# Attention input of a graph transformer: expert rows added to x inside the gather transfers, in two groups of eight, with two x buffers

## The reference, cut to what matters

```
x = x + gnn0(layernorm(x), adj)
x = x + moe(layernorm(x))           # a shared expert + the top 2 of 8 experts per node
x = x + attention_gnn(layernorm(x), adj)
x = x + slicing_attention(layernorm(x))

# attention_gnn, 4 heads of 32:
X, q, k = heads(leaky(x @ W_lin + b)), heads(leaky(x @ W_q)), heads(leaky(x @ W_k))
adj_h = adj * sigmoid(q k^T / sqrt(32));  deg = sum(adj_h, -1)
dis = where(deg > 0, deg ** -0.5, 0)
Y = dis * adj_h * dis @ X;  out = layernorm(Y) * ln_g + ln_b
```

## Time and profile before

| | |
|---|---|
| median of 3 runs | 1789.09 us (1788.44 to 1789.14) |
| the profiled execution's own time | 1787.95 us |
| its span | 1786.2 us |
| TensorE, VectorE busy | 1534.8 us, 1054.1 us of the span |
| ScalarE, GpSimd busy | 702.1 us, 717.3 us |
| mean granted TensorE clock | 0.928 of full speed |
| attention stage in the span | from about 730 to 1330 us |

### The profile page before, as it was taken

One profiled execution on the slowest core, in us unless ns is written; L12 is line 12 of the kernel. 1 busy time (PEld: TensorE's weight loads), 2 busy tenths in 40 slices (PEclk: granted clock), 3 DMA queues, 4 the chain that ended last, 5 costly groups with the idle time before them and its releaser, 6 DMA issues. The chain is left out here.

```text
span 1786.2 us, 25017 instructions
## 1 busy us (share of the span) xinstructions
PE 1534.8 (86%) x9208; PEld 834.3 (47%) x9208; DVE 1054.1 (59%) x2248; ACT 702.1 (39%) x978; POOL 717.3 (40%) x501
## 2 busy tenths in 40 slices
PE   5899997996999999237999989999958999967598
PEld 2355555655766677212222222222215777743278
DVE  2467774411232222139899989998957887825612
ACT  3365645332333333025555545556502343412110
POOL 1137776400000000379878777842225565610000
PEclk9899998998999999669999999999977898979799
DMA  9676643555555554223334333333220000020214
GB/s 281 219 254 218 210 133 93 163 128 135 151 146 141 142 151 120 73 82 114 113 100 125 99 108 115 104 106 97 83 61 24 22 15 23 1 84 1 47 56 136
DMA packets 214663, 199.86 MB, mean 112 GB/s; under 512 B 22529, under 2 KB 176513, under 8 KB 214546
## 3 DMA queue, kind: packets, MB, share of 16 engines
q1 hardware_dynamic: 206354, 181.46, 34.4%
q0 software_dynamic: 8192, 16.86, 2.9%
HBM read 150.17 MB, written 48.10 MB: 111 GB/s over the span
## 5 line engine op out<-in xcount | busy, mean ns | idle before, releaser
L1249 DVE TENSOR_TENSOR c_AH<-c_AH,c_A 128x2048 f32<-128x2048 f32 x128 | 314.9, 2469 | 38.5 <-ACT c_AH L1218 37.7
L1218 ACT ACTIVATE c_AH<-c_S 128x2048 f32<-128x2048 f32 x128 | 240.6, 1880 | 226.4 <-PE c_S L1116 226.4
L687 ACT ACTIVATE a_A<-a_DG,a_A 128x512 f32<-128x512 f32 x220 | 150.7, 687 | 275.8 <-PE a_DG L561 271.2
L1065 POOL DMA_INDIRECT c_G<-ys,slots x128 | 223.7, 1748 | 44.1 <-issue 41.0
L561 PE MATMUL a_DG<-a_A 128*128 128x512 f32 x440 | 216.3, 615 | 7.0 <-ACT a_A L687 7.0
L1116 PE MATMUL c_S<-c_Q,c_K 32*128 32x512 f32 x1024 | 151.5, 662 | 23.8 <-DVE c_K L1306 12.9
L444 POOL DMA_INDIRECT rows<-a_S,a_slots x128 | 134.6, 1051 | 56.2 <-issue 42.9
L1049 POOL MEMSET c_power<- 128x32 f32 x1 | 0.1, 124 | 388.5 <-issue 388.5
L1141 PE MATMUL c_DG<-c_AH,c_ones 128*32 128x512 f32 x1024 | 139.9, 619 | 16.4 <-DVE c_AH L1249 16.3
L1129 PE MATMUL c_YA<-c_AH,c_XT 128*32 128x512 f32 x1024 | 137.1, 617 | 7.2 <-DVE c_XT L1274 7.2
L561 PEld LDWEIGHTS a_DG<-a_A 128*128 128x128 f32 x440 | 75.7, 192 | 107.1 <-ACT a_A L687 79.0
(11 more groups left out here) (314 smaller groups left out, 2413.1 us busy)
## 6 DMA issues: line engine op xcount, KB each, us to landing
a_A<-in_dram SPq DMA_DIRECT2D x32, 1024.0 KB, 9.7
c_A<-in_dram SPq DMA_DIRECT2D x128, 256.0 KB
a_A<-in_dram SPq DMA_DIRECT2D x40, 514.0 KB, 3.4
a_A<-rows SPq DMA_DIRECT2D x39, 258.0 KB, 3.7
ys<-a_A SPq DMA_DIRECT2D x39, 256.0 KB, 2.3
rows<-a_zero SPq DMA_DIRECT2D x16, 258.0 KB, 9.2
a_X<-in_dram SPq DMA_DIRECT2D x8, 512.0 KB, 13.3
a_R<-in_dram SPq DMA_DIRECT2D x8, 512.0 KB, 4.7
```

The source lines that it names most:

```text
L687: act.activation(hT[g % 2][:, f, :], UP[f % 2], ACT.Gelu, bias=w_of(g)[:, F_N + f:F_N + f + 1]).then_inc(h_ready, 1)
L1065: pool.indirect_dma_start(Gt[k][:, t, :], None, ys, bass.IndirectOffsetOnAxis(ap=slots[:, k, T * i + t:T * i + t + 1], axis=0), bounds_che ...
L1218: act.activation(AH[g % UNITS][:, :, :], S[:, :, :], ACT.Sigmoid, scale=HD ** -0.5).then_inc(att_ready, 1)
L1249: dve.tensor_tensor(ah[:, :, :], ah[:, :, :], A[g % ADJ_BUFS][:, :].unsqueeze(1).to_broadcast([P, HEADS, HALF]), ALU.mult).then_inc(ah_dve, 1)
```

## The change

Each gather adds the rows that it fetches to X in the transfer (`compute_op=ALU.add`). `Gt` and the two additions of `combine` are gone. A transfer that adds reads X and writes it back, so the eight gathers of a graph's first expert wait for the load of X, and the eight of the second expert wait for the first eight. X has two buffers, taken in turn, each with its own semaphores for loading and storing; `load_x(i + 2)` moves from step 11 to step 1, and the loads of graphs 0 and 1 stand first in SP's queue. On GpSimd the first eight gathers of graph i + 2 stand after root(i - 1, 1), the second eight after root(i, 0). VectorE's statistics and `keep_x` wait for the sixteen gathers where they waited for the addition.

```diff
-        X, Y, R = sb("X", [P, T, D]), sb("Y", [P, T, D]), sb("R", [P, T, D])
-        Gt = [sb(f"G{k}", [P, T, D]) for k in range(2)]
+        X = [sb(f"X{u}", [P, T, D]) for u in range(2)]
+        Y, R = sb("Y", [P, T, D]), sb("R", [P, T, D])
...
             def load_x(i):
-                if i > 0:
-                    sp.wait_ge(side_full, full["xn1", i - 1])
-                sp.dma_start(X[:, :, :], tiled(x_in[i])).then_inc(x_loaded, 16)
+                if i >= 2:
+                    sp.wait_ge(side_full, full["xn1", i - 2])
+                sp.dma_start(X[i % 2][:, :, :], tiled(x_in[i])).then_inc(x_loaded[i % 2], 16)
 
             def keep_x(i):
-                sp.wait_ge(x_ready, i + 1)
-                sp.dma_start(tiled(kept[i]), X[:, :, :]).then_inc(x_kept, 16)
+                sp.wait_ge(gathered, 256 * i + 256)
+                sp.dma_start(tiled(kept[i]), X[i % 2][:, :, :]).then_inc(x_kept[i % 2], 16)
 
             load_x(0)
+            load_x(1)
             for g in range(2):
                 load_adj(g)
             keep_x(0)
-            load_x(1)
...
-                    if n == 11 and is_graph(i + 2):
+                    if n == 1 and is_graph(i + 2):
                         load_x(i + 2)
...
-            def gather(i, part):
+            def gather(i, k, part):
                 if is_graph(i):
-                    wait(pool, x_ready, i)
-                    for m in part:
-                        k, t = divmod(m, T)
+                    pool.wait_ge(x_loaded[i % 2], 16 * (i // 2 + 1))
+                    wait(pool, gathered, 256 * i + 128 * k)
+                    for t in part:
                         pool.indirect_dma_start(
-                            Gt[k][:, t, :], None, ys,
+                            X[i % 2][:, t, :], None, ys,
                             bass.IndirectOffsetOnAxis(ap=slots[:, k, T * i + t:T * i + t + 1], axis=0),
-                            bounds_check=limit).then_inc(gathered, 16)
-
-            def combine(i):
-                pool.wait_ge(gathered, 256 * i + 256)
-                pool.tensor_tensor(Gt[0][:, :, :], Gt[0][:, :, :], Gt[1][:, :, :], ALU.add).then_inc(pair_ready, 1)
-                pool.wait_ge(pair_ready, i + 1)
-                pool.wait_ge(x_loaded, 16 * i + 16)
-                pool.tensor_tensor(X[:, :, :], X[:, :, :], Gt[0][:, :, :], ALU.add).then_inc(x_ready, 1)
-
-            gather(0, range(16))
-            combine(0)
+                            bounds_check=limit, compute_op=ALU.add).then_inc(gathered, 16)
+
+            gather(0, 0, range(T))
+            gather(0, 1, range(T))
             norm_in.power(pool, power, 0, 0)
-            gather(1, range(16))
-            combine(1)
+            gather(1, 0, range(T))
+            gather(1, 1, range(T))
             for i in range(B + 2):
-                gather(i + 2, range(4))
                 if is_graph(i + 1):
                     norm_in.power(pool, power, i + 1, (i + 1) % 2)
                 if is_graph(i - 1):
                     root(i - 1, 1)
-                gather(i + 2, range(4, 8))
+                gather(i + 2, 0, range(T))
                 if is_graph(i - 2):
                     pool.wait_ge(r_loaded, 16 * (i - 1))
                     pool.tensor_tensor(R[:, :, :], R[:, :, :], wide(shift), ALU.add).then_inc(shifted, 1)
                     norm_y.power(pool, power, i - 2, i % 2)
-                gather(i + 2, range(8, 16))
                 if is_graph(i):
                     root(i, 0)
-                if is_graph(i + 2):
-                    combine(i + 2)
+                gather(i + 2, 1, range(T))
...
             def stats_x(i):
-                dve.wait_ge(x_ready, i + 1)
-                norm_in.stats(dve, X, i, i % 2)
+                dve.wait_ge(gathered, 256 * i + 256)
+                norm_in.stats(dve, X[i % 2], i, i % 2)
 
             def apply_x(i):
-                dve.wait_ge(x_kept, 16 * i + 16)
-                norm_in.apply(dve, X, X, i, i % 2).then_inc(xn_ready, 1)
+                dve.wait_ge(x_kept[i % 2], 16 * (i // 2 + 1))
+                norm_in.apply(dve, X[i % 2], X[i % 2], i, i % 2).then_inc(xn_ready, 1)
```

More of the change, by code:

```diff
@@ L971, in attention_gnn_stage @@
         w_loaded, consts = sem("w_loaded"), sem("consts")
-        x_loaded, r_loaded, stored = sem("x_loaded"), sem("r_loaded"), sem("stored")
+        x_loaded = [sem(f"x_loaded{u}") for u in range(2)]
+        r_loaded, stored = sem("r_loaded"), sem("stored")
         adj_loaded = [sem(f"adj_loaded{b}") for b in range(ADJ_BUFS)]
@@ L975, in attention_gnn_stage @@
         norm_y = LayerNorm(lambda n, s: sb("y" + n, s), lambda n: sem("y" + n))
-        gathered, pair_ready, x_ready, x_kept = sem("gathered"), sem("pair_ready"), sem("x_ready"), sem("x_kept")
+        gathered = sem("gathered")
+        x_kept = [sem(f"x_kept{u}") for u in range(2)]
         xn_ready = sem("xn_ready")
@@ L1159, in side @@
                     for c in range(4):
-                        mm = pe.transpose(M[:, c * P:(c + 1) * P], X[:, 4 * half + c, :], ident[:, :])
+                        mm = pe.transpose(M[:, c * P:(c + 1) * P], X[i % 2][:, 4 * half + c, :], ident[:, :])
                 elif what[:-1] == "x":
```

## The result

The changed kernel takes 1810.53 us (median of 4 runs, 1807.26 to 1811.95) against 1789.12 before: a ratio of 1.0117, 95% interval 1.0100 to 1.0135. It is 1.2% slower. The forecast was 1779, faster; what came is rival (a), a dear adding gather, just inside the range. The profiled execution took 1810.76 us with a span of 1809.0, against 1787.95 and 1786.2.

The account below looks back on a forecast made before the run. TensorE sets a steady round's pace, 61.9 us, and GpSimd's additions cost about 6 us more through VectorE. Terms -25.4 + 0 - 2.7 + 15.6 + 2.0 = -10.5 us gave 1779 us, range 1764 to 1812.

Parts of the forecast that it names:

- rival (a): GpSimd's adding gathers issue 0.2 us or more above plain ones; 1802 us at 1.5; 33% together with slow landing.
- the price of an adding gather: GpSimd's issue of each adding gather: 1.05 us assumed, between bounds 1.01 and 2.06; +2.0 us in all.
- the estimate of 1.5 us: Issue time of one adding gather if it goes with the moves; the sum would come out at 1802 us.
- The additions: GpSimd's two additions for each graph block VectorE; removing them from six rounds gives -25.4 us.
- The start: Inputs of the first two graphs, gathered in two groups of eight: 0 us for graph 0, -2.7 us for graph 1.
- The order: Second eight gathers behind root(i, 0): VectorE stalls 5.5 us, TensorE loses 2.6 in each of six rounds, +15.6 us.
- Rival (b): In the rounds the gathers are in time or VectorE's idleness takes the whole stall: no +15.6, 1763 us; chance 15%.
- (c): No stall is absorbed, as TensorE also waits at side products: 17.4 us more, 1796 us; chance 12%.
- The price in the rounds: Each us more for an adding gather costs about 3.2 us in each of the six VectorE stalls.
- The sum: All terms over the whole kernel: -25.4 + 0 - 2.7 + 15.6 + 2.0 = -10.5 us.
- The shift's addition and root(i - 1, 1): On GpSimd, the addition now behind eight gathers and root(i - 1, 1) before them: cost 0 us.

Follow-up runs that it names:

- second_early: The changed kernel with all of the second eight gathers moved ahead of root(i, 0); 1798 us.
- spread: The changed kernel with the gather order of the kernel before, x of graph i + 3 being loaded at step 11; 1791.20 us.
- plain_price: The changed kernel with plain gathers in the same places and with the same waits, overwriting x instead of adding; 1777.65 us.

## Why the prediction was wrong

The step that failed is the price of an adding gather. I took 1.05 us because two forms of indirect DMA in the trace cost nearly the same, and neither of them adds. It is 1.56, 0.55 above a plain one; the prediction put the point from which this rival decides at 0.25. The Trainium skill (Collectives: The Full Stack, Stop ④ — SDMA + CCE) shows two reads and a write for an add; the estimate of 1.5 us that was worked out from it stands close to the 1.56 measured, its 1802 us 8.5 below the time. That issue time goes with the moves is not shown by this: it is one agreement, and nothing here varies the moves alone. The estimate was left out of the sum, and that was the weighing that went wrong: an operation in no row was priced by rows that share only its name.

Point by point, from the marks:

- **The additions**, -25.4 us forecast. 20.7 in the rounds (533.95 to 513.29). The block of VectorE is as forecast, but that four fifths came is in part luck. The sum counted each blocked us once, in every round; in the rounds of graphs 1, 2 and 5 only 1.0 to 1.9 us came, and of the 20.7 TensorE's idle time gave 11.3. The other 9.3 are its products at a higher granted clock, a term that the sum did not have.
- **The start**, -2.7 forecast. With plain gathers in the same order the marks say -4.5 (793.13 for 797.58), counted from the load of x -1.7: right in kind and near in size. The price adds 17.3 us counted so, and 32 x 0.55 = 17.6 is the issue alone: all of it is issue, as far as one profile of each can tell. +15.6 in all, +14.5 by the marks.
- **The order**, +15.6 forecast. At the plain price 529.34 - 513.29 = 16.1 us. The stall of VectorE, 5.5 forecast, was 3.8 to 5.2 in five of six rounds, and TensorE's waits behind them 1.0 to 2.6, 10.1 together, where 6 x 2.6 had been forecast; 4.6 of the 16.1 are longer busy time of TensorE (468.83 for 464.21). So the near agreement is in part luck as well. second_early and spread show by undoing it that the stall comes from the place of the gathers behind root(i, 0). Rival (b), no stall, falls with that, and (c), nothing absorbed, with the slack of 1.8 to 2.8 us in each stall.
- **The price in the rounds**, 19 us for each us: 10.5 expected for 0.55, 13.0 measured (542.36 less 529.34), of which 4.7 are again TensorE's busy time.
- **The sum** with 1.56 put in would have been -25.4 - 2.7 + 15.6 + 51 x 0.55 = +15.6 us; measured were +21.4 between the medians and +22.9 at the stage end. Most of the rest is what the additions' gain lacked (4.7) and the price in the rounds had more (2.5). In rival (a) the step from 1.05 to 1.5 us is written as 0.46 and is 0.45; 1802 stands.
- The shift's addition and root(i - 1, 1) were taken as free. No wait of VectorE names them in the steady rounds of the changed kernel, but a block shows as a longer instruction, not as a wait. In three of the four steady rounds the addition lengthens the output norm's step to 4.29 us from 2.18, much as it had lengthened the input's normalisation before. In round 3 it meets a leaky step (0.69 us elsewhere), and TensorE waits for the multiply behind it:

```profile
1025.93 3.74 DVE L1298 SCALAR_TENSOR_TENSOR c_XR<-c_XR 128x512 f32<-128x512 f32 x1
1026.23 2.88 POOL L1085 TENSOR_TENSOR c_R<-c_R,c_shift 128x1024 f32<-128x1024 f32 x1
1031.93 1.66 PE L1133 MATMUL c_DG<-c_AH,c_ones 128*32 128x512 f32 x8 [2.63 <-DVE c_AH L1241]
```

What stays open: the three marks rest on one profile each, so parts under about 2 us are not certain, and how much of TensorE's longer busy time each wait brings was not followed. Whether the 0.55 us are spent on reading the destination or on preparing a further transfer a row was not tried; no kernel here separates them.

What the Trainium skill (SBUF — State Buffer, Who interferes with whom) infers, that a multiply with two SBUF inputs does not hinder the issue of gathers, does not hold here. In the changed kernel, too, a gather that begins under a multiply takes 2.92 us (1128.55, above) where 1.56 is its price, and in the kernel before each of the 60 gathers that begin well inside one takes 1.67 us or more. Whether the gather's own read of `slots` in SBUF is what meets the multiply, no run here separates. An adding gather ends 1.43 us after the multiply, a plain one 0.89, so the 0.55 us are paid there as well.

## What to carry to other kernels

An addition moved into a transfer was not free here: it was paid where the transfer is issued, 0.55 us by the instruction, and in series at the start, where nothing else is to be waited for. So do it in the steady rounds, where the issuing engine has slack, and not at a start, where an idle engine does the same work in 1.23 us. When gathers take over an addition, keep the date by which they must have landed and place them before that date, not where the addition stood. A wait of TensorE can cost more than its length: look at the products behind it and at their granted clock. And do not price an operation that no row shows by its nearest relative in name: put it in the sum between its bounds, or time it first.

## What the runs showed of the hardware beyond that

The adding gathers are cut into more packets. The profile page's line of the queue on which GpSimd's DMAs run, of the kernel before and then of the changed one, with the same bytes:

```profile
q0 software_dynamic: 8192, 16.86, 2.9%
```

```profile
q0 software_dynamic: 22528, 16.86, 5.2%
```

The difference is 14336 packets on 128 gathers: 112 more for each, and the share of the DMA engines' time goes up by 2.3 points. That is no limit here, and a landing took hardly longer (1.8 us after 1.67; the gap between two groups of eight 2.60 for 2.22 in plain_price), so what an adding gather costs in this kernel is nearly all GpSimd's time to issue it.
